# V as the second kind with its test beside Q, the K sums of s in four quarters of the array, one power for rows and u, and a new order of flag, gather, branch and x1

## The reference, cut to what matters

```python
xn = _layernorm(x)
x = x + gnn(xn, edges) + mix(xn[None])[0]
x = x + ffn(_layernorm(x)[None])[0]          # all rows are one sample

def gnn(xn, (row, col)):                     # 4 heads of 64
    xt = xn @ weight
    alpha = softmax over heads of leaky_relu(attn_l . xt[row] + attn_r . xt[col])
    return sum over heads of alpha[:n] * xt[col[:n]], repeated to 256 columns

def mix(x):                                  # c = 1
    h = relu(batchnorm(conv(logmap0(proj(x)), w_qkv)))     # 768 channels, statistics over all rows
    t = logmap0(proj(proj(expmap0(h))))
    s = conv(conv(t, w_dw), w_pw, 24 groups of 32)
    t2 = logmap0(proj(proj(expmap0(cat(t, s)))))
    q, k, v = t2 in groups of 96, split by 32;  q, k = relu(q), relu(k)
    vk  = einsum(v, k) per row and group
    out = einsum(vk, q) / (sum(v) + 1e-15)
    return proj(expmap0(conv(logmap0(proj(expmap0(out))), w_res) + b_res))

def ffn(x):
    weights = softmax of the router on the mean of the rows; the top 2 of 8 experts
    return layernorm(sum of w_e * (gelu(x @ W1[e] + b1[e]) @ W2[e] + b2[e]) + x)
```

## Time and profile before

| | |
|---|---|
| median of three runs | 845.83 us (845.48 to 846.97) |
| profiled execution | 845.97 us, span 844.2 us |
| TensorE matmul busy | 782.3 us (93%) |
| TensorE weight load busy | 639.6 us (76%) |
| VectorE busy | 523.2 us (62%) |
| ScalarE busy | 424.8 us (50%) |
| GpSimd busy | 388.5 us (46%) |
| mean granted TensorE clock | 0.964 |

### The profile page before, as it was taken

How to read it: one execution, slowest core, us unless ns; L and a number is a source line. 1 busy time by engine, 2 the same in 40 slices (tenths; PEclk the granted TensorE clock), 3 DMA queues, 4 the chain that set the end, 5 groups by cost and what they waited for, 6 DMA issues and landing times. The chain is left out here.

```text
span 844.2 us, 14806 instructions
## 1 busy us (share of the span) xinstructions
PE 782.3 (93%) x4938; PEld 639.6 (76%) x4938; DVE 523.2 (62%) x1475; ACT 424.8 (50%) x959; POOL 388.5 (46%) x601
## 2 busy tenths in 40 slices
PE   5899999998799999999669679999999999999996
PEld 4678888887366667766436568888888888888885
DVE  7762488797578888888888643534444353535345
ACT  2466436888578888888548232223231323222230
POOL 2430878877068888887636601312222221312122
PEclk9899999999699999999969879999999999999999
DMA  8755122222011110211101040000000000000000
GB/s 215 189 157 147 41 59 57 53 51 52 7 50 44 53 60 21 64 43 53 41 7 33 19 125 13 16 22 21 17 25 13 25 12 25 13 25 14 25 20 30
DMA packets 35421, 41.31 MB, mean 49 GB/s; under 512 B 11520, under 2 KB 20696, under 8 KB 35339
## 3 DMA queue, kind: packets, MB, share of 16 engines
q1 hardware_dynamic: 22355, 30.71, 12.7%
q0 software_dynamic: 8000, 6.82, 3.7%
q10 hardware_dynamic: 4984, 2.79, 1.3%
HBM read 25.59 MB, written 14.60 MB: 48 GB/s over the span
## 5 line engine op out<-in xcount | busy, mean ns | idle before, releaser
L916 ACT ACTIVATE Z<-ps,b1s 128x250 f32<-128x250 f32 x200 | 93.8, 469 | 234.6 <-PE ps L1140 234.6
L1153 PE MATMUL ps<-Z 128*125 128x256 f32 x800 | 176.5, 379 | 0.0
L1140 PE MATMUL ps<-Z 128*128 128x250 f32 x800 | 175.0, 376 | 1.2 <-DMA Z<-in_w 1.2
L1140 PEld LDWEIGHTS ps<-Z 128*128 128x128 f32 x800 | 152.6, 191 | 19.8 <-DMA Z<-in_w 1.6
L1153 PEld LDWEIGHTS ps<-Z 128*125 128x125 f32 x800 | 150.1, 188 | 22.3
L978 PE MATMUL ps<-Z,L 128*128 128x250 f32 x600 | 126.9, 373 | 0.0
L651 POOL TENSOR_SCALAR zr<-zmv 125x1 f32<-125x1 f32 x50 | 11.1, 221 | 250.1 <-issue 240.3
L978 PEld LDWEIGHTS ps<-Z,L 128*128 128x128 f32 x600 | 113.6, 189 | 13.2
L1728 DVE TENSOR_TENSOR Z<-ps,L 125x256 f32<-125x256 f32 x50 | 21.2, 425 | 161.1 <-PE ps L1153 161.1
L1077 PE MATMUL ps<-wr,Z 128*125 128x256 f32 x400 | 92.6, 384 | 0.0
L774 ACT ACTIVATE Z<-Z,bn_o,bn_s 128x250 f32<-128x250 f32 x150 | 80.7, 599 | 1.5 <-DVE bn_o L1439 1.5
(11 more groups left out here) (212 smaller groups left out, 1261.6 us busy)
## 6 DMA issues: line engine op xcount, KB each, us to landing
Z<-in_x SPq DMA_DIRECT2D x25, 250.0 KB
out<-Z SPq DMA_DIRECT2D x24, 250.0 KB
xt_table<-L SPq DMA_DIRECT2D x25, 231.0 KB
Z<-in_x SPq DMA_DIRECT2D x1, 2016.0 KB
g_table<-gt SPq DMA_DIRECT2D x25, 62.5 KB
gr<-g_table SPq DMA_DIRECT2D x25, 62.5 KB
Z<-in_x SPq DMA_DIRECT2D x1, 1344.0 KB
Z<-in_w SPq DMA_DIRECT2D x2, 512.0 KB, 3.7
```

The lines of the kernel that those rows point to most:

```text
L916: a_.activation(ge[:, b % 2, f, :], ps[:, f % 4, 0:BT], ACT.Gelu, bias=b1s[:, f // NF, f % NF:f % NF + 1]).then_inc(gelu_done.sem, 1)
L1140: last = mm(ps[:, f % 4, 0:BT], w1s[:, f // NF, k, (f % NF) * 128:(f % NF + 1) * 128], h_of(b, k), start=(k == 0), stop=(k == KD - 1))
L1153: last = mm(ps[0:TP, 4 + 2 * (b % 2) + t, 0:D], ge[:, b % 2, f, t * TP:(t + 1) * TP], w2s[:, f // NF, f % NF, :], start=(f == 0), stop=(f ...
```

## The change

The order of kinds becomes K, V, Q. Stage 2 then has the statistics of V early, so the early relus are those of K and of 20 blocks of V (`EARLY_V`), and the relus left for stage 3 are all those of Q and V's last five. `check_t` for these 20 blocks moves from stage 3 into stage 2's loop on VectorE: 19 of them from n = 56 on, the 20th behind `edge_sums`; its result has a column for each block (`chkt`), and `check_s` adds it in, so the checks are three columns instead of four. In stage 3 block 0's V is made ahead of its Q and K.

The products of `pointwise_v` and `k_sums_s` go to other places: the two halves of K are kept differently (h = 0 with its quarters swapped, h = 1 not), results of V and the K sums of t share banks 3 and 4, and the K sums of s go to banks 1 and 2, in all four quarters. Because halves now lie in different banks, V's square and the products of VectorE take their operands from two banks, `attend_t` waits for all three squares, and the branch swaps halves of its divisor with two copies, and divides with three products instead of two. The weights and constants follow: 24 small copies of the batchnorm's numbers on VectorE instead of 12, and 4 more short ones on ScalarE.

GpSimd's `rstd_of_x1` and the power in `scale_of_u` become one function, `powers(k)`: one power for the row variances of block k - 1 and u's squares of block k. `make_xn` waits for it. Its order in a step becomes flag (ahead of the last scale of u), last scale, scale of norms, gather, edge block (from 2 on), `powers`, `scale_of_u`, edge block (below 2). On VectorE the branch stands ahead of `make_x1`, and `attend_s` ahead of `check_s` and `attend_t`.

h is kept at column 0 of its block's area instead of 4·BT, and the router's small table `rt` lies in an area of another array.

```diff
-        KINDS = (R_K, R_Q, R_V)
-        EARLY_RELU, EARLY_Q = 30, 20
-        assert EARLY_RELU + NB + EARLY_Q == 3 * NB
+        KINDS = (R_K, R_V, R_Q)
+        EARLY_RELU, EARLY_V = 30, 20
+        assert EARLY_RELU + NB + EARLY_V == 3 * NB
...
+            def powers(k, rows_=True, u_=True):
+                a = k % 2
+                if rows_:
+                    wait_apart(pool, x1, x1.count(k - 1))
+                    g.tensor_scalar(pin[0:TP, a, 0], mv2[0:TP, k - 1, :, 1], LN_EPS, None, ALU.add).then_inc(var_made.sem, 1)
+                if u_:
+                    wait_apart(pool, u_sq, u_sq.count(k))
+                    g.tensor_scalar(pin[0:TP, a, 1], us[0:TP, a], MIN_NORM ** 2, None, ALU.max).then_inc(sq_made.sem, 1)
+                if rows_:
+                    pool.wait_ge(var_made.sem, var_made.count(k - 1))
+                if u_:
+                    pool.wait_ge(sq_made.sem, sq_made.count(k))
+                js = slice(0 if rows_ else TB, 2 * TB if u_ else TB)
+                powered = rows_pow if rows_ else u_pow
+                g.tensor_tensor(rsu[0:TP, k].rearrange("p r t -> p (r t)")[:, js], pin[0:TP, a].rearrange("p r t -> p (r t)")[:, js],
+                                nhalf[0:TP, js], ALU.pow).then_inc(powered.sem, 1)
             def scale_of_u(b):
                 if b >= 2:
                     pool.wait_ge(x1.sem, x1.count(b - 2))
-                wait_apart(pool, u_sq, u_sq.count(b))
-                g.tensor_scalar(s[:, 0], us[0:TP, b % 2], MIN_NORM ** 2, None, ALU.max).then_inc(n.sem, 1)
-                pool.wait_ge(n.sem, n.count(b, 1))
-                g.tensor_tensor(s[:, 1], s[:, 0], nhalf[0:TP, 0:TB], ALU.pow).then_inc(n.sem, 1)
-                pool.wait_ge(n.sem, n.count(b, 2))
-                g.tensor_tensor(s[:, 2], s[:, 0], s[:, 1], ALU.mult).then_inc(n.sem, 1)
+                pool.wait_ge(*made_of_u(b))
+                g.tensor_tensor(sg[0:TP, b % 2, 0], pin[0:TP, b % 2, 1], rsu[0:TP, b, 1], ALU.mult).then_inc(scale_g.sem, 1)
...
-            def rstd_of_x1(b):
-                wait_apart(pool, x1, x1.count(b))
-                g.tensor_scalar(vr[0:TP, b % 2], mv2[0:TP, b, :, 1], LN_EPS, None, ALU.add).then_inc(rstd_done.sem, 1)
-                pool.wait_ge(rstd_done.sem, rstd_done.count(b, 1))
-                g.tensor_tensor(rstd2[0:TP, b], vr[0:TP, b % 2], nhalf[0:TP, 0:TB], ALU.pow).then_inc(rstd_done.sem, 1)
...
             steps(NB, [
+                (1, raise_flag),
                 (3, last_scale_of_u),
-                (1, raise_flag),
                 (1, scale_of_norms),
+                (2, gather_piece),
                 (2, lambda b: add_edge(b) if b >= 2 else None),
-                (3, rstd_of_x1),
+                (2, lambda b: powers(b, rows_=b > 0)),
                 (2, scale_of_u),
-                (2, gather_piece),
                 (2, lambda b: add_edge(b) if b < 2 else None),
             ])
+            raise_flag(NB - 1)
             last_scale_of_u(NB - 3)
-            raise_flag(NB - 1)
             scale_of_norms(NB - 1)
             add_edge(NB - 2)
-            rstd_of_x1(NB - 3)
+            powers(NB - 2)
             scale_of_u(NB - 2)
             scale_of_norms(NB)
             last_scale_of_u(NB - 2)
             add_edge(NB - 1)
+            powers(NB - 1, rows_=False)
             scale_of_u(NB - 1)
             last_scale_of_u(NB - 1)
-            rstd_of_x1(NB - 2)
-            rstd_of_x1(NB - 1)
+            powers(NB - 1, u_=False)
+            powers(NB, u_=False)
...
+            relu(0, R_Q, relu_q)
+            square_s(0, R_V)
             square_t(0)
...
-                (0, ahead(lambda b: relu(b, R_Q, relu_q) if b >= EARLY_Q else None)),
-                (0, ahead(lambda b: relu(b, R_V, relu_v))),
+                (0, ahead(lambda b: relu(b, R_Q, relu_q))),
+                (0, ahead(lambda b: relu(b, R_V, relu_v) if b >= EARLY_V else None)),
                 (1, square_o),
-                (0, lambda b: square_s(b, R_V)),
+                (0, lambda b: square_s(b, R_V) if b else None),
...
-                    pe.wait_ge(att.sem, att.count(b - 1, 1))
+                    pe.wait_ge(att.sem, att.count(b - 1, 2))
                 else:
-                    pe.wait_ge(z_kept.sem, 3 * NB - 4)
+                    pe.wait_ge(z_kept.sem, 3 * NB - 3)
+                    pe.wait_ge(relu_k.sem, relu_k.count(0))
+                    pe.wait_ge(pw_made, NC)
+                    pe.wait_ge(bo_made, 9)
                 for h in range(NH):
                     cv, ck = 2 * R_V + h, 2 * R_K + h
                     for a in range(2):
-                        last_v = quarter(bank_half(R_V, h), pw[:, cv, :], zc(b, cv), a, a)
-                        last_k = quarter(bank_half(3, h), bo, zc(b, ck), a, 1 - a)
-                last_v.then_inc(s_done.sem, 1)
+                        last_v = quarter(bank_half(4 - h, 1), pw[:, cv, :], zc(b, cv), a, a ^ h)
+                        last_k = quarter(bank_half(3 + h, 0), bo, zc(b, ck), a, 1 - (a ^ h))
+                last_v.then_inc(v_done.sem, 1)
                 last_k.then_inc(kst_done.sem, 1)
             def k_sums_s(b):
                     pe.wait_ge(att.sem, att.count(b - 1))
                 else:
                     pe.wait_ge(z_kept.sem, 3 * NB)
-                for h in range(NH):
-                    for a in range(2):
-                        last = quarter(bank_half(4, h), bo, skr[:, h * BT:(h + 1) * BT], a, a)
-                last.then_inc(kss_done.sem, 1)
+                for a in range(2):
+                    last_0 = quarter(bank_half(1, 0), bo, skr[:, 0:BT], a, a)
+                    last_1 = quarter(bank_half(2, 0), bo, skr[:, BT:2 * BT], a, 1 - a)
+                last_0.then_inc(kss_done.sem, 1)
+                last_1.then_inc(kss_done.sem, 1)
...
+                (0, lambda b: None if b else pointwise_v(b)),
                 (0, pointwise_kq),
                 (1, turn_norms),
                 (2, res),
                 (4, turn_xn),
-                (0, pointwise_v),
+                (0, lambda b: pointwise_v(b) if b else None),
                 (0, k_sums_s),
                 (0, norms),
...
+            def check_t(b):
+                dve.wait_ge(relu_v.sem, relu_v.count(b))
+                if b:
+                    dve.wait_ge(t_checked.sem, t_checked.count(b - 1))
+                if b > EARLY_V:
+                    dve.wait_ge(checked.sem, checked.count(b - 1))
+                v_.scalar_tensor_tensor(out=junk, in0=zc(b, 2 * R_V, 2), scalar=TINY, in1=zc(b, 2 * R_V, 2), op0=ALU.is_lt,
+                                        op1=ALU.mult, accum_out=chkt[:, b:b + 1]).then_inc(t_checked.sem, 1)
             for n in range(3 * NB):
...
+                    check_t(n - 1 - EARLY_RELU - NB)
             bn_variance(2)
             edge_pair(EARLY // 2 - 1)
             bn_affine(2)
             edge_sums(EARLY // 2 - 1)
+            check_t(EARLY_V - 1)
...
             def attend_t(b):
                 dve.wait_ge(kst_done.sem, kst_done.count(b))
-                dve.wait_ge(s_done.sem, s_done.count(b, S_KQ))
+                dve.wait_ge(s_done.sem, s_done.count(b))
                 dve.wait_ge(t_sq.sem, t_sq.count(b))
+                dve.wait_ge(s_sq.sem, s_sq.count(b))
                 if b:
                     dve.wait_ge(att.sem, att.count(b - 1))
-                v_.scalar_tensor_tensor(out=vk, in0=zc(b, 2 * R_V, 2), scalar=0.0, in1=ps[:, 3, 0:2 * BT],
+                v_.scalar_tensor_tensor(out=pair(vk), in0=pair(zc(b, 2 * R_V, 2)), scalar=0.0, in1=ps[:, 3:5, 0:BT],
                                         op0=ALU.is_gt, op1=ALU.mult).then_inc(att.sem, 1)
-                dve.wait_ge(att.sem, att.count(b, 1))
+                dve.wait_ge(att.sem, att.count(b, 2))
                 v_.tensor_tensor(ob(b, 0, 2), vk, zc(b, 2 * R_Q, 2), ALU.mult).then_inc(att.sem, 1)
             def attend_s(b):
                 dve.wait_ge(q_kept.sem, q_kept.count(b))
                 dve.wait_ge(kss_done.sem, kss_done.count(b))
-                v_.tensor_tensor(ob(b, 2, 2), ps[:, 4, 0:2 * BT], sqr, ALU.mult).then_inc(att.sem, 1)
+                v_.tensor_tensor(pair(ob(b, 2, 2)), ps[:, 1:3, 0:BT], pair(sqr), ALU.mult).then_inc(att.sem, 1)
             def check_s(b):
                 a = b % 2
                 dve.wait_ge(s_sq.sem, s_sq.count(b))
-                dve.wait_ge(checked.sem, checked.count(b, 1))
-                v_.tensor_scalar(junk, sqs[:, R_V], TINY_SQ, 0.0, ALU.is_lt, ALU.add,
-                                 accum_out=chk[:, a, 1:2]).then_inc(checked.sem, 1)
+                dve.wait_ge(t_checked.sem, t_checked.count(max(b, EARLY_V - 1)))
+                if b:
+                    dve.wait_ge(checked.sem, checked.count(b - 1))
+                if b >= 2:
+                    dve.wait_ge(flag_done.sem, flag_done.count(b - 2))
+                v_.tensor_scalar(junk, sqs[:, R_V], TINY_SQ, chkt[:, b:b + 1], ALU.is_lt, ALU.add,
```

(11 more changed lines are left out.)

137 lines of the change are left out of this document (74 added, 63 removed).

## The result

The changed kernel takes 851.08 us (median of 6 runs, 850.27 to 854.52) against 845.90 for the kernel before: a ratio of 1.0069 with a 95% interval of 1.0052 to 1.0086. It is slower by about 5.2 us. The prediction said 848.4, slower, with a range to 852.0.

A forecast was written before the change was run, and what follows sets the result against it. Four engines were taken as close to the bound, with K's sums and V's square ending together. Terms -0.4 + 2.25 - 0.8 + 0.4 + 0 + 1.1 = +2.55 us on 845.97 gave 848.4 us after 0.14 less; range 843.5 to 852.0.

The forecast's parts named there:

- the debt of the checks: Moved checks on VectorE ahead of the third variance, before the block loop: 6.0 us too many, variance near 214.4 us.
- Four quarters: Block loop: second sums over K halve, but norms still wait for V's square; -0.4 us over 18 steps.
- the saving's arrival: Rival, block loop: V's square is ready before the sums over K end; 841.2 us, chance 0.10.
- Block 0: Start of the block loop: V needs no late statistics and its square leaves the chain; -1.1 us.
- Steps 1 to 4: Early block loop repays delay: -0.6 us in step 1, -2.15 us in steps 3 and 4 by the earlier flag.
- Branch ahead of x1: Block loop, VectorE's order: ScalarE gets the branch sooner and two TensorE stalls go; -0.8 us, bounds -1.2 and +3.
- One power: Block loop, GpSimd: with powers joined make_xn waits for u's squares, late softmax slips in five steps; +0.4 us.
- the ring rival: Rival, block loop: GpSimd and VectorE form a ring longer than TensorE's step; +3.5 us, 851.9 us, chance 0.20.
- Branch taken: The one step taking the branch: earlier start against two copies and one more product; 0 us, bounds -1 and +1.
- Tail: Behind the loop: make_xn(22) waits for the joined power, and all behind it is serial up to the router; +1.1 us.

The follow-up runs named there:

- the split wait: Changed kernel, norms waiting for the square of V only ahead of their third group of sums: 848.61 us; same edit in the kernel before: 844.32 us.
- the run with the powers apart: Changed kernel with two powers again, for rows and for u, the rows' first, make_xn waiting for that alone: 850.09 us.
- the spread checks: Fast kernel with 12 checks of t beside Q's projection and 8 at the end of VectorE's steps 0 to 2: 837.65 us; in the changed kernel 851.23 us.
- the fast kernel: Changed kernel with two powers again and norms waiting for the square of V only ahead of their third group: 839.39 us.

## Why the prediction was right, and where not

The direction held, and so did the main mechanism: the debt of the checks, and a saving of the quarters that the square of V keeps from the time. 851.08 lies in the range, 0.9 us from its end. But the sum reached +2.55 us and the change cost 5.2, and that it was not further off is in part luck, since errors in both directions met. Term by term:

*Four quarters, predicted -0.4, measured about +1.1.* Right that the saving is lost to the square of V. Mis-sized by the handover: V's square now reads two banks and waits for the K sums of t beside V, and starts 0.54 us behind V's last group instead of 0.43. The semaphores in the two traces say which of the two it is: V's own signal comes 0.40 us behind the start of that group in both, the K sums' 0.04 later, and the square begins 0.08 behind this second one, where it began 0.02 behind V's alone. So about 0.10 of the 0.11 us come with the second wait; no run tried it without, nor the two banks alone. The steady step became 0.08 us longer, not 0.02 shorter, 14 times. That wait was named in none of my steps. What lay behind the square wasn't named either: I put the saving's arrival at 841.2 us if the square were ready, and the split wait showed that it would still not have come.

*The debt, predicted 6.0, measured 4.4.* The third variance began at 214.54 us where I had said 214.4:

```profile
184.31 0.74 DVE L1361 BATCH_NORM_STATS2 L<-Z 128x6 f32<-128x250 f32 x2
184.96 0.66 DVE L1488 SCALAR_TENSOR_TENSOR L<-Z 128x500 bf16<-128x500 f32 x1
185.55 0.08 DVE L1488 DVE_READ_ACCUMULATOR L<-Z 128x1 f32 x1
185.55 0.73 DVE L1361 BATCH_NORM_STATS2 L<-Z 128x6 f32<-128x250 f32 x2
214.54 0.49 DVE L1469 BATCH_NORM_AGGREGATE bmv<-bpart 128x2 f32<-128x36 f32 x2
```

That agreement is partly luck: the whole program was 1.5 us late by then. From one power to the next the debt is 4.44 us. The step that failed is the price of a check: I took 0.68 us from its start to the next instruction in the earlier trace rows, but here the next one starts 0.59 us after (185.55 - 184.96; 0.59 to 0.60 for all 19), the instructions overlapping more. 19 x 0.09 = 1.7 us is the whole difference. An absolute time that fits is no proof of a term; the stretch between two marks is.

*Block 0, predicted -1.1, measured -1.4* (4.97 - 6.36). V as the second kind does what it should.

*Steps 1 to 4, predicted -2.75, measured -1.6.* Step 1 gave 0.53 of 0.6, step 3 0.74 of 0.9 (V had waited 0.82 there against a steady step, not 0.9), step 4 only 0.40 of 1.25. V no longer waited in step 4, but the norms did. The timeline of that step, GpSimd, VectorE and ScalarE:

```profile
254.99 1.41 POOL L612 TENSOR_TENSOR Z<-Z,gr 125x256 f32<-125x256 f32 x2 [0.91 <-DMA gr<-g_table]
255.03 0.70 DVE L1412 TENSOR_TENSOR at<-asrc,xg 125x8 f32<-125x8 f32 x1
255.77 0.65 DVE L1414 SCALAR_TENSOR_TENSOR at<-at 125x8 f32<-125x8 f32 x1
256.35 0.37 POOL L589 CROSS_LANE_REDUCE flag<-chk 128x1 f32<-128x3 f32 x1
256.85 0.21 ACT L884 ACTIVATE at<-at 125x8 f32<-125x8 f32 x1 [1.79 <-DVE at L1419]
```

The edge block of b = 1, which had stayed in front of the flag, waited for its transfer. Two small products of VectorE beside it took 0.70 and 0.65 us and not their 0.17, so the late softmax came late, and ScalarE waited 1.79 us with the squares behind it. In the run with the powers apart both products came just ahead of the edge block and took 0.17 us each; the exponential behind them stood 3.02 us into the step instead of 3.73, and the step took 9.43 us instead of 10.14, the same 0.71 less. I had noted that this edge block stays in front and gave it no price. The Trainium skill, in "SBUF — State Buffer" (Who interferes with whom), says that a VectorE instruction with two SBUF inputs and a GpSimd one that reads SBUF exclude each other; the prediction had read from the trace only GpSimd's power held by VectorE; here the trace shows VectorE held by GpSimd, for L1412 and L1414 end 0.02 us behind the two halves of the edge block (255.74 and 255.71, 256.42 and 256.39).

*Branch ahead of x1, predicted -0.8, measured 0* (steps 5 to 20: 149.61 and 149.68 us with x1 on either side). Of the two waits that I meant to save, the one near 340 us goes with GpSimd's order alone (0.56 to 0.20 us in that run), and the one near 453 us stayed (norms 1.14 us behind the start of the last K sum, 0.79 in a steady step).

*One power, predicted +0.4, measured 0.1 in the loop.* This is the case of an edit that is free under another wait: beside the split wait it costs 149.38 - 141.62 = 7.8 us. The place where it hurts, `make_xn`, then `keep_turned` and the late softmax, was named; that it was the next bound of all was the ring rival's point. But that rival named its path as GpSimd's total work, and this alone was not it: with the powers apart GpSimd does more, 121.1 us in 142, and steps are 8.78. My own reason, that `make_xn` now waits for u's squares as well, isn't it either: in the run with the split wait GpSimd waited for these squares in 2 of 16 steps, 1.1 us in all. What the traces show instead is where the power ends. The joined one has a second input ahead of it (0.3 us) and takes 1.0 to 1.5 us instead of 0.73, so the value for `make_xn` comes 1.1 us later behind the edge block in the two steps shown above.

*Branch taken, predicted 0 with bounds of 1, measured +1.05*; 28.32 us with x1 first too, so the place of x1 isn't the cause. The traces show what is. The same 16 small copies of VectorE in the branch, before and after, with what stands ahead of them and beside them in the changed kernel:

```profile
415.54 4.05 DVE L1537 COPY L<-ebt 32x64 f32<-32x64 f32 x16
417.90 0.16 DVE L1575 TENSOR_TENSOR et<-nrm,npw 125x2 f32<-125x2 f32 x1 [1.05 <-POOL npw L598]
419.02 5.55 DVE L1583 COPY L<-ebt 32x64 f32<-32x64 f32 x16
418.88 1.35 POOL L577 DMA_INDIRECT xg<-xt_table,idst  x1 [0.29 <-issue]
420.27 1.40 POOL L612 TENSOR_TENSOR Z<-Z,gr 125x256 f32<-125x256 f32 x2
```

The branch began 1.19 us earlier in its step, but its first instruction waited 1.05 us for the norms' power, so 0.30 was gained (4.96 us into the step instead of 5.26). Then the copies took 1.50 us more: one ran from 419.23 to 421.05, 1.82 us instead of 0.19, until the first half of the edge block had ended (421.00), and the next took 0.65. With GpSimd's new order alone, in the kernel before, they take 5.37 us, so it is the gather, now ahead of the edge block, that lengthens them. The two copies and the third product cost 0.70. V's products came 1.90 us later, and the rest of the step was 0.85 shorter; between profiles of the changed kernel and its variants that rest varies from 5.35 to 6.23 us. I had priced the copies and the product, took an earlier start as a gain, and had no term for GpSimd beside the branch. *Tail, predicted +1.1, measured +1.36*, of which powers apart give back 1.04.

Taken together: three terms came out cheaper than priced (debt 1.6, one power 0.3, block 0 0.3) and five dearer (quarters 1.5, steps 1 to 4 1.15, branch 0.8, branch taken 1.05, tail 0.25): 2.55 us net. The table has 2.1 more than the sum (4.65 - 2.55); the 0.4 between them were gained in the late steps, where GpSimd's new order alone, in the kernel before, took 0.8 us off steps 5 to 20 (148.96 to 148.19). One reading was off without consequence: ten steps between 265 and 410 us have 9.20 us, not 12.

## What to carry to other kernels

When an operation on the bounding engine gets shorter, look up which waits stand at its end, and split or move the one that ends with it in the same edit; then look for the next one, since 12 us appeared here only when two waits were loosened together, worth 2.5 and 1.0 us alone by the medians. Joining two small operations saves time on their engine but makes the first consumer wait for both inputs and for the longer operation: price it by the consumer, with the present bound taken away. Where work is moved away from one wait, look up which path it stands on then: the spread checks gave back 1.8 of 2.8 us in the step behind them. And measure a term between two marks in the trace, not at an absolute time: the first 127 us of this kernel alone vary by 6 us from one execution to another.

## What the runs showed of the hardware

A check of 128x500 (0.66 us in its record) keeps the next VectorE instruction waiting for 0.59 us beside `bn_stats` in the projection stage and 0.68 in the block loop. Small two-input operations of VectorE took 0.65 to 0.70 us instead of 0.17 while GpSimd added an edge block, and a copy of 32x64 took 1.82 us instead of 0.19 beside a gather and the first half of an edge block. A power on GpSimd took 0.73 us for 125x2 in the fast kernel and 1.03 for 125x4 in the changed one (medians). The signal of V's products came 0.40 us behind the start of their last group in most steps and 0.57 to 0.67 in others; in the step looked at nothing differs in the records ahead of it, and the next group's signals are not late. That one is unexplained.
